# Decoder steps with gates and batch on partitions, 128x8 cell operations, the encoder term written to PSUM ahead of the convolution, and one alignment store

## The reference

```
conv   = conv1d(alpha_prev, conv_w)          # 10 filters of 101 taps over 128 positions
e      = va . tanh(Wa_s s + (Wa_h h + ba) + Wa_f conv)   # 128 positions
alpha  = softmax(e, masked beyond the row's length)
g      = sum_t alpha[t] * h[t]               # context, 256
rec    = L_ys y_t + L_ss s + L_gs g + b      # 512: four gates of 128
i,f,o  = sigmoid(...), c~ = tanh(...)
c      = f * c + i * c~ ;  s = o * tanh(c)
```

## Time and profile before

| | us |
|---|---|
| median of 3 runs | 4213.84 (4213.58 to 4214.56) |
| the profiled execution's own time | 4207.08 |
| its span, first to last instruction | 4205.3 |
| the decoder's loop, first to last L1952 | 2197.6 to 3716.5 |
| TensorE, VectorE, ScalarE busy over the span | 3526.3, 2660.2, 1564.5 |

### The profile page before, as it was taken

The page is one execution under the profiler, slowest core; times in us unless marked ns, Lnnn a source line. Parts: engine busy times, 40 slices in busy tenths (PEclk is TensorE's granted clock), DMA queues, the critical chain, the costliest instruction groups (busy, mean ns, idle before and its releaser), DMA issues. The chain is left out here.

```text
span 4205.3 us, 66878 instructions
## 1 busy us (share of the span) xinstructions
PE 3526.3 (84%) x21282; PEld 1828.8 (43%) x21354; DVE 2660.2 (63%) x6647; ACT 1564.5 (37%) x3710; POOL 504.9 (12%) x1854
## 2 busy tenths in 40 slices
PE   6546478444599999995989999999999999974998
PEld 4424155222376777772533333333333333322554
DVE  2665767588655555553227777777777777764443
ACT  2221144354322222221115555555555555532222
POOL 0000511233200010000000000000000000023222
PEclk9566689777799999998999999999999999976888
DMA  2000020200100000001013233333233233211000
GB/s 92 3 2 8 2 46 8 83 0 0 42 1 0 0 0 0 0 0 51 15 39 82 78 81 82 78 82 82 78 82 82 78 82 82 78 33 46 25 25 30
DMA packets 272180, 176.49 MB, mean 42 GB/s; under 512 B 17054, under 2 KB 258216, under 8 KB 272056
## 3 DMA queue, kind: packets, MB, share of 16 engines
q1 hardware_dynamic: 269368, 172.54, 14.4%
q0 software_dynamic: 2752, 3.18, 0.5%
HBM read 164.94 MB, written 13.90 MB: 43 GB/s over the span
## 5 line engine op out<-in xcount | busy, mean ns | idle before, releaser
L1783 PE MATMUL ps<-st_hk,de_wct 112*128 112x512 f32 x1024 | 525.9, 595 | 14.3 <-DVE st_lss L1903 13.1
L1849 ACT ACTIVATE st_th<-st_pre,st_sw 128x128 f32<-128x128 f32 x1024 | 327.2, 390 | 552.7 <-DVE st_sw L1908 552.7
L1804 PE MATMUL ps<-de_hg,st_at 128*32 128x512 f32 x4096 | 492.5, 598 | 0.3 <-DVE st_at L1939 0.3
L1922 DVE SCALAR_TENSOR_TENSOR st_th<-ps,st_sw,de_enc 128x128 f32<-128x128 f32 x1024 | 288.5, 345 | 30.1 <-DVE st_sw L1908 0.4
L1798 PE MATMUL ps<-st_lss,st_sT 128*128 128x512 f32 x512 | 288.1, 645 | 0.0
L1952 DVE TENSOR_TENSOR st_rec<-ps,st_rin 128x256 f32<-128x256 f32 x512 | 193.3, 418 | 125.9 <-PE ps L1804 125.9
L1783 PEld LDWEIGHTS ps<-st_hk,de_wct 112*128 112x128 f32 x1024 | 189.1, 205 | 140.5 <-DMA st_hk<-padded_alignments 72.2
L1764 POOL COPY de_ah<-st_at 128x8 f32 (+1 forms) x256 | 51.0, 199 | 1656.6 <-DVE st_at L1939 1656.6
L1247 PE MATMUL ps<-sa_xt,w_wq 128*128 128x128 f32 x2048 | 237.9, 278 | 1.9 <-ACT sa_xt L1363 1.9
L1247 PEld LDWEIGHTS ps<-sa_xt,w_wq 128*128 128x128 f32 x2048 | 234.7, 194 | 11.0 <-issue 9.2
L1318 PE MATMUL ps<-sa_wo,sa_ct 128*128 128x512 f32 x512 | 225.0, 598 | 13.1 <-issue 13.1
(11 more groups left out here) (402 smaller groups left out, 6412.7 us busy)
## 6 DMA issues: line engine op xcount, KB each, us to landing
st_hk<-padded_alignments SPq DMA_DIRECT2D x508, 224.0 KB, 3.2
X<-in_x_dram SPq DMA_DIRECT2D x16, 512.0 KB, 12.0
out_dram<-X SPq DMA_DIRECT2D x16, 512.0 KB, 2.7
padded_alignments<-st_al SPq DMA_DIRECT2D x508, 2.0 KB
w_wq<-in_Wq_perm_dram SPq DMA_DIRECT2D x1, 4096.0 KB, 18.0
sa_wo<-in_Wo_perm_dram SPq DMA_DIRECT2D x1, 4096.0 KB, 14.5
gate_inputs<-dp_ro SPq DMA_DIRECT2D x16, 256.0 KB, 2.0
st_rin<-gate_inputs SPq DMA_DIRECT2D x256, 16.0 KB
```

The costliest lines, as they stand in the source:

```text
L1783: pe.matmul(ps[:, CV[g] + i, :], wct[:, :], hk[g][:, 4 * i:4 * i + 4, :].rearrange("p b n -> p (b n)"), start=True, stop=True).then_inc(co ...
L1804: ins = pe.matmul(R[g][32 * j:32 * j + 32, :], at[g][:, j, i, :], hg[:, BG * g + 4 * i + j, :], start=False, stop=(i == 1), tile_position= ...
L1849: ins = act.activation(th[g][:, b, :], pre[g][:, b, :], ACT.Tanh, bias=sw[g][:, b:b + 1])
L1922: ins = dve.scalar_tensor_tensor(out=th[g][:, b, :], in0=ps[:, CV[g] + 1, (b - 4) * P:(b - 3) * P], scalar=sw[g][:, b:b + 1], in1=enc[:, B ...
```

## The change

- The gates' product is turned by quarters. A quarter of the array now belongs to one gate (`q`), and each of the 8 rows gives four products of 128 columns: `gates_of_context` is 32 products of 128 columns (L1814) in place of 8 of 512, and `gates_of_state` is 4 products of 128 columns (L1807) in place of one of 512. The stationary operand has the row's alignment in one of 32 columns (`at`: 128 x 8 x 32).
- The sum is 128x128 (gate and batch on partitions, unit along the free dimension). After the gate inputs are added, TensorE transposes it (`turn_gates`, L1820) and ScalarE takes the tanh of 32 columns. The cell operations are 128x8, and the new state is written where the next products read it, with no transposition and no copy from PSUM. The factor 0.5 of the state goes into the weights `lss`, `was` and, in the stage behind, `lsy`.
- The encoder term is copied into the convolution's two PSUM banks by VectorE ahead of it (`fill`, L1931), and the convolution adds to it. ScalarE reads the first bank; VectorE adds the state term to the second in one instruction (L1937).
- The order of TensorE's half is new: first convolution, state term, turned alignment, second convolution, context, state gates, mask, first energies, turned gates, second energies. `turn_alignment` and `keep_alignment` move from the end of the front part to the start of the back part.
- The alignment is stored in one transfer of eight rows, and the gate inputs are loaded in one transfer instead of two.

```diff
@@ TensorE @@
                     def half(g, n, o, m, u, more):
                         front = not isinstance(m, int) or m <= LAST
                         if front:
+                            convolve(o, m, 0)
                             state_term(o, m)
+                        turn_alignment(g, n)
+                        if front:
+                            convolve(o, m, 1)
                         gates_of_context(g, n)
                         if front:
-                            energy(o, m)
                             gates_of_state(o, m)
-                        if more:
-                            convolve(g, n + 1, 0)
+                            mask(o, m)
+                            energy(o, m, 0)
+                        turn_gates(g, n)
                         if front:
-                            turn_alignment(o, m)
-                        if more:
-                            pe.wait_ge(s_rows[g], n + 1)
-                            pe.transpose(ST[g], s2[g][:, :], ident[:, :]).then_inc(st_ps[g], 1)
-                            convolve(g, n + 1, 1)
+                            energy(o, m, 1)
...
                     def gates_of_state(g, n):
-                        pe.matmul(R[g], sT[g][:, :], lss[:, :], start=True, stop=False, skip_group_check=True)
+                        for q in range(4):
+                            pe.matmul(R[g][32 * q:32 * q + 32, :], sT[g][:, :], lss[:, q * P:(q + 1) * P],
+                                      start=True, stop=False, tile_position=(0, 32 * q), skip_group_check=True)
...
-                        for i in range(2):
-                            for j in range(4):
-                                ins = pe.matmul(R[g][32 * j:32 * j + 32, :], at[g][:, j, i, :], hg[:, BG * g + 4 * i + j, :],
-                                                start=False, stop=(i == 1), tile_position=(0, 32 * j), skip_group_check=True)
+                        for b in range(BG):
+                            for q in range(4):
+                                ins = pe.matmul(R[g][32 * q:32 * q + 32, :], at[g][:, b, :], hg[:, BG * g + b, q * P:(q + 1) * P],
+                                                start=False, stop=(b == BG - 1), tile_position=(0, 32 * q), skip_group_check=True)
...
+                    def turn_gates(g, n):
+                        pe.wait_ge(rec_ready[g], n + 1)
+                        pe.transpose(T[g], rec[g][:, :], ident[:, :]).then_inc(t_ps[g], 1)
@@ ScalarE @@
-                        for i in range(2):
-                            act.wait_ge(rec_ready[g], 2 * n + i + 1)
-                            act.activation(gt[g][:, 2 * P * i:2 * P * (i + 1)], rec[g][:, 2 * P * i:2 * P * (i + 1)],
-                                           ACT.Tanh).then_inc(gates_done[g], 1)
+                        act.wait_ge(t_ps[g], n + 1)
+                        act.activation(gt[g][:, :], T[g][:, 0:128:4], ACT.Tanh).then_inc(gates_done[g], 1)
@@ VectorE @@
+                    def fill(g, n, i):
+                        dve.wait_ge(th_done[g], 2 * n) if not (isinstance(n, int) and n == 0) else dve.wait_ge(cleared, 4)
+                        dve.tensor_copy(CV[g][i], enc[:, BG * g + 4 * i:BG * g + 4 * i + 4, :].rearrange("p b n -> p (b n)")).then_inc(filled[i][g], 1)
+                    def add_state(g, n):
+                        dve.wait_ge(conv_ps[1][g], n + 1)
+                        dve.wait_ge(sw_ready[g], n + 1)
+                        dve.tensor_tensor(th[g][:, 4:8, :], rows4(CV[g][1]), sw[g][:, 4:8].unsqueeze(2).broadcast_to([P, 4, P]),
+                                          ALU.add).then_inc(added[g], 1)
...
                         dve.wait_ge(tc_done[g], n + 1)
-                        dve.scalar_tensor_tensor(out=s2[g][:, :], in0=to, scalar=1.0, in1=tc[g][:, :], op0=ALU.add,
-                                                 op1=ALU.mult).then_inc(s_rows[g], 1)
                         if more:
-                            add_encoder(g, n + 1)
-                        if front:
-                            keep_alignment(o, m)
-                        if more:
-                            dve.wait_ge(st_ps[g], n + 1)
                             dve.wait_ge(hist_s[g], n + 1)
-                            dve.tensor_scalar(sT[g][:, :], ST[g], 0.5, None, ALU.mult).then_inc(st_ready[g], 1)
+                            dve.scalar_tensor_tensor(out=states(g), in0=to, scalar=1.0, in1=tc[g][:, :], op0=ALU.add,
+                                                     op1=ALU.mult).then_inc(st_ready[g], 1)
@@ SyncE @@
-                        for i in range(2):
-                            r0 = BG * o + 4 * i
-                            sp.dma_start(pad_d.ap()[r0:r0 + 4, PADA:PADA + P], al[o][i:128:32, :]).then_inc(al_out[i][o], 16)
+                        sp.dma_start(pad_d.ap()[BG * o:BG * o + BG, PADA:PADA + P], al[o][0:128:16, :]).then_inc(al_out[o], 16)
+                        sp.wait_ge(al_out[o], 16 * m + 16)
                         for i in range(2):
-                            sp.wait_ge(al_out[i][o], landed)
                             sp.dma_start(hk[o][:, 4 * i:4 * i + 4, :], hankel(o, i)).then_inc(hk_in[i][o], 16)
```

More of the change, by code:

```diff
@@ L1684, in stage_decoder @@
+            CV = [[ps[:, 4 * g + i, :] for i in range(2)] for g in range(G5)]
+            R = [ps[:, 4 * g + 2, 0:P] for g in range(G5)]
+            T = [ps[:, 4 * g + 2, P:2 * P] for g in range(G5)]
             E = [ps[:, 4 * g + 3, 0:P] for g in range(G5)]
             AT = [ps[:, 4 * g + 3, P:2 * P] for g in range(G5)]
[L1686 removed]
             SW = [ps[:, 4 * g + 3, 3 * P:3 * P + BG] for g in range(G5)]
[L1688 to L1689 removed]
+            SETUP = 19
@@ L1701, in cols, with by_batch, states, rows4 @@
-            def cols(v):
-                return v.rearrange("p (j c) -> p c j", c=32)[:, 0:2, :]
+                f = v[:, :, :].rearrange("p b c -> p (b c)")
+                return bass.AP(f.tensor, f.offset, [list(f.ap[0]), [36 * 4, 2], [36, 4]])
+            def by_batch(v):
+                return v.rearrange("p (j i c) -> p i j c", i=2, c=16)[:, :, :, 0]
+            def states(g):
+                return sT[g][:, 0:32:4]
+            def rows4(v):
+                return v.rearrange("p (b n) -> p b n", n=P)
@@ new lines, in mask, with energy @@
+                    def mask(g, n):
+                        pe.wait_ge(sw_ready[g], n + 1)
+                        pe.matmul(E[g], ident16[:, :], mask16[:, g, :], start=True, stop=False, skip_group_check=True)
+                    def energy(g, n, i):
+                        pe.wait_ge(th_done[g], 2 * n + i + 1)
+                        for j in range(4):
+                            ins = pe.matmul(E[g][32 * j:32 * j + 32, :], vas[:, i, :], th[g][:, 4 * i + j, :],
+                                            start=False, stop=(i == 1), tile_position=(0, 32 * j), skip_group_check=True)
+                        if i == 1:
+                            ins.then_inc(e_ps[g], 1)
@@ L1832, in _ @@
                         for i in range(2):
-                            convolve(g, 0, i)
+                            pe.matmul(CV[g][i], wct[:, :], hk[g][:, 4 * i:4 * i + 4, :].rearrange("p b n -> p (b n)"),
+                                      start=True, stop=True).then_inc(cleared, 1)
+                    for i in range(2):
+                        convolve(0, 0, i)
                     state_term(0, 0)
-                    energy(0, 0)
                     gates_of_state(0, 0)
-                    turn_alignment(0, 0)
+                    mask(0, 0)
+                    for i in range(2):
+                        energy(0, 0, i)
                     steps(pe, half)
@@ L1945, in half @@
                             keep_state_term(o, m)
-                            add_all(o, m)
-                        dve.wait_ge(r_sum[g], n + 1)
-                        dve.wait_ge(rin_in[u // 2][g], 32 * state["it"] + 32)
-                        for i in range(2):
-                            half_of = slice(2 * P * i, 2 * P * (i + 1))
-                            dve.tensor_tensor(rec[g][:, half_of], R[g][:, half_of], rin[g][:, u, half_of],
-                                              ALU.add).then_inc(rec_ready[g], 1)
+                        keep_alignment(g, n)
+                        if more:
+                            fill(g, n + 1, 0)
+                        if front:
+                            add_state(o, m)
+                        if more:
+                            fill(g, n + 1, 1)
+                        dve.wait_ge(r_sum[g], n + 1)
+                        dve.wait_ge(rin_in[u // 2][g], 16 * state["it"] + 16)
+                        dve.tensor_tensor(rec[g][:, :], R[g], rin[g][:, u, :], ALU.add).then_inc(rec_ready[g], 1)
                         if front:
                             top(o, m)
-                        dve.wait_ge(gates_done[g], 2 * n + 1)
```

(6 more changed lines are left out.)

118 lines of the change are left out of this document (47 added, 71 removed).

## The result

The changed kernel takes 4264.85 us (median of 4, 4255.80 to 4267.14) against 4213.71 us for the kernel before beside it (4208.75 to 4214.56): a ratio of 1.012, interval 1.0102 to 1.0137. It is 51 us slower; 39 was forecast.

The account below looks back on a forecast made before the run. TensorE's work bounds the half, VectorE's chain ending within 0.04 us; a half grows from 5.95 to 6.11. 256 x 0.16 = 41, less 2, is +39: 4246 from 4207.1, 4253 with the median's 6.8; range 4190 to 4330.

Parts of the forecast that it names:

- the signs named ahead: Profile after: state term's load waits some 0.6, half 6.1, context and state gates 2.0; a convolution waiting for transfer contradicts.
- the reserve: TensorE's wait for the state in each half, 0.62 us, which could absorb alignments landing 0.11 late.
- a half's 0.16: Loop: each half grows from 5.95 to 6.11 us; 256 of them add 41 us.
- the turned gates with their second switch: TensorE between first and second energies: 0.11 plus 0.10 for a second switch, to 4.17 in the half.
- the gain outside the loop: Set-up and other parts outside the loop, mainly fewer gate-input buffers to clear: together -2 us, ends -3 and +1.
- A switch at 0.10: TensorE: each change between whole array and quarters costs 0.10 us of emptying the array; five in the chain.
- The rival that lived on cheaper switches: TensorE's chain: two free switches give a 5.91 half and 4202 us, all free 5.61 and 4125; chance 0.17.
- The upward bound: VectorE's cell and state operations: four 128x8 ones at 0.29 each add 0.48 a half, or 123 us.
- Rounds of 128 columns: Context and state gates: 0.11 a round; rival says they don't keep up, 6.65 a half, 4391 us, or 4760; chance 0.08.
- Late alignments: Convolution's transfers: rival says landing at 4.2 instead of 3.2 adds 0.25 a half, 4317 us; chance 0.05.
- Instruction list: TensorE's loop list grows from some 710 to some 1,590 instructions; rival of instruction fetches, chance 0.05.
- The two-page rule: TensorE's loop: a taken branch out of a window of two 16 KB pages stalls for a fetch.

Follow-up runs that it names:

- the extra operation: Changed kernel with one more 128x128 operation on a spare tile on VectorE ahead of the three cell operations: 4259.31 us, ratio 1.0116.
- both convolutions in the tail: Changed kernel with the second convolution moved up, so both stand ahead of the state term: 4251.16 us, ratio 1.0103 to the kernel before.
- the mask on quarters: Changed kernel with the mask's product as four products of 32 columns instead of one on the whole array: 4464.97 us, ratio 1.0598.

## Why the prediction was right, point by point

**Direction and mechanism.** The cause named was the chain through the maximum, which now holds the turned gates and a convolution while one convolution covers its tail. The timeline has it step by step. Counted from the state term's load, as said and as measured: context 1.34 and 1.34, mask 3.45 and 3.44, first energies 3.61 and 3.61, turned gates 3.96 and 3.96, second energies 4.17 and 4.22, maximum 4.66 and 4.71, reciprocal 5.44 and 5.53, state 5.89 and 5.93, half 6.11 and 6.15. Taking the turned gates from between the energies, alone, turned 51 us more than before into 42 less (4167.61 against 4209.57 beside it). Of the signs named ahead, two did not come as written. The load of the state term waited 1.1, not 0.6, and the array itself 0.22 on the mean. And the convolution did wait for its transfer, which the forecast had called a sign of being wrong; since its own sum had that wait inside the reserve, the sign was put too strictly, and the halves of 6.14 to 6.16 show that the chain set the pace all the same.

**The size, 51 for 39.** The step from a half's 0.16 to 41 us was the one off: the half grew by 0.20 (6.158 less 5.957), or 51.5 us. The term that was mis-sized is the turned gates with their second switch, put at 0.21 and measured at 0.26 (2507.70 to 2507.96); it moves all that follows by 0.05. The reciprocal comes another 0.04 later, since it waits for the exp (2508.78 to 2509.24, 0.46 for 0.44, and 0.03 of hand-over), and from there to the state it is 0.40 in place of 0.45, which gives that back. What is left net of these is this 0.05, less 0.01: 10 of the 12 us. The other 2 are the gain outside the loop, which doesn't show in the start of the loop.

**The unit prices.** A switch at 0.10, inferred from sums of pieces, was about right: two with a mask of four small products in place of one gave 0.23 a half, some 0.11 each, and two with a transposition gave 0.38. The rival that lived on cheaper switches is out.

**The cell operations.** The 128x8 form takes 0.16 to 0.17, as taken from the copy. Two independent ones start 0.08 apart, so all end at 2509.10, well before the exp, and the reciprocal waits 0.17 for the exp. The forecast had them as the last to end, by 0.10; that end of the chain was read wrongly and cost little, since the exp is nearly as late. The upward bound (0.29 each, 123 us) was never near, as the extra operation showed.

**Rounds of 128 columns.** From the context's first matmul to that of the state gates it is 1.77 (2505.08 to 2506.85) for 16 rounds: 0.11 a round, and load to load from the context to the mask is 2.10. So the rounds kept up over 18 although all work on the same rows of the array. The rule of the Trainium skill weighed in the forecast (TensorE: Matmul & The Clock Gate, Part 3, The mechanism), that a weight load overlaps running matmuls only when the row groups differ, would have given 6.65 a half; 6.158 decides against it in this case. (The same section also lets a load go ahead into a background weight buffer, which would fit the rows; no run here shows that buffer.)

**Late alignments.** Said 0.11 late with 0.62 in reserve (the terms as given, 5.92, 1.59 and 3.2, add up to 10.71, which is 0.08 late). Measured, the convolution's load waits for its transfer in 131 of 211 halves, 0.40 each, the load in the shown half 0.15 behind its forecast place, and the idle left behind it is 0.36 there, 0.22 on the mean. The 0.62 is smaller by the 0.15 of lateness and by 0.15 that the convolution took longer by the trace's modelled end (1.12 for 0.97), and larger by the 0.04 of the longer half. The reserve held, but is smaller than said; where it is gone, the transfers bound (both convolutions in the tail).

**Instruction list.** Nothing is fetched in the loop of the changed kernel, 1,585 instructions long: this rival did not strike. Its price was wrong, though: 1 to 3 us a turn said, 8 measured where it struck. The two-page rule (the Trainium skill, Runtime: NRT & Kernel Launch, Instruction fetch mechanics) would have had the changed loop fetch in each turn; 41 packets in the whole run say no. The same section gives TensorE an instruction memory of 2,048 instructions, by which both lists fit; that holds for 1,585 at three places and fails for 1,633 at one of two. That a loop can be fetched again in each turn is what the mask on quarters shows.

**Cover that cost nothing.** The fills are off the path, as said, by the run with fills of 8 columns; the gate sum behind them still waits 0.62 for its products.

## What to carry to other kernels

Work taken from an engine that is busy but not waited for buys nothing; what counts is what stands between the last common input and the result that starts the next half. On TensorE, order products so that the result that VectorE waits for comes first, and keep products of one tile shape together: each change of shape cost 0.11 us here, and a reorder of one line was worth twice what the change lost. When a long unrolled loop turns suddenly slow by some per cent, look at the packets of instructions and at the waits on issue before looking for a cause in what the edit computes.

## What was not expected of the hardware

- A loop of 1,633 TensorE instructions was fetched again each turn (about 9 packets of 16 KB, 8 us a turn), and not when it stood 100 instructions further on. The granted clock, 1.00 in the changed kernel, was 0.93 on the mean: in the shown place it was 1.00 up to 2639, 0.50 from 2643 to 2647, behind a gap of 4.38 us, and 1.00 again behind 2651.
- Small VectorE operations that don't depend on each other overlap: 0.08 apart at 0.16 long, while a dependent one follows 0.19 later (2508.74 to 2508.93).
- Halving the transferred copies, with both convolutions in the tail, gave 80 us where I had expected 49. The array's wait for transfers, 0.25 a half, accounts for 64 of them (0.25 x 256); the whole loop got 74 shorter (6.092 to 5.803 a half), and what gave the rest was not tried.
